# Gate and up products of an adaLN block's feed-forward: seven block products in place of eight, with its copies, splits and loads in a new order

## The chip, the core and the metric

One core of a Trainium2 chip runs the whole kernel in one launch. The metric is device time in microseconds (us), the median of three runs. The engines are PE (TensorE: matrix products, and PEld, its weight loads), DVE (VectorE), ACT (ScalarE), POOL (GpSimd) and SP (SyncE, which issues the DMAs). Each engine works through its own list of instructions in order; semaphores hold an instruction until another engine has signalled. SBUF is the on-chip memory of 128 partitions; PSUM, where PE puts its results, has 8 banks of 128 x 512 float32.

## The reference, cut to what matters

Four sequences of 512 tokens of width 512 go through an attention part (a gated delta rule with 6 heads) and then a feed-forward part:

```python
x = x + ga * attention(h)                       # h: normed, modulated x
h = _layernorm(x, axis=-1) * (1 + cb) + sb
gate = jnp.einsum('bsd,hd->bsh', h, w_gate)     # 2048 hidden units, 512 inputs
up   = jnp.einsum('bsd,hd->bsh', h, w_up)
gated = jax.nn.silu(gate) * up
x = x + gb * jnp.einsum('bsh,dh->bsd', gated, w_down)
```

All is float32. Both kernels make a float32 product out of three faster ones (type fp32r): each operand is split into a high part (a copy rounded to fp32r, made by ACT) and a low part (operand minus high part, made by DVE or POOL), and high x high, low x high and high x low are added up in one PSUM bank.

## The kernel before

**Order.** The program is a list of steps (`plan`), which each engine's function walks through, taking the parts that are its own. So the order of the `step(...)` calls is the order of every engine's list. Three stages matter here: projections and convolutions (to about 310 us of the trace), sixteen *units* of the recurrence (`slot_of(u)`, u = 0 to 15, to about 505 us), and the feed-forward.

**Units.** A unit works on 64 tokens of two sequences (`place(u)` gives the pair of sequences p and the chunk c; units 0, 1, 4, 5, 8, 9, 12, 13 belong to p = 0). Its output side is `po_sq`, `po_ln`, `po_os` (norm of the heads), `po_tr` (turn, gate, split), `po_wo` (18 matmuls by Wo), `po_yg`, `po_add`, `po_stat`, `po_xn`, which gives `XN1`, the normed rows for the feed-forward. SP writes them to `scrN` and the sum itself to `scrX`. PSUM banks 4 to 7 are handed out in two pairs by `take()` in turn.

**Feed-forward.** Hidden units are cut into 16 tiles j of 128; tokens into the four sequences b. For each j and b, `gu_gate` and `gu_up` are 4 x 3 matmuls each into one of banks 0 to 3 (`mm3`, line 1304): 64 x 24 = 1536 matmuls of 512 columns. ACT takes silu of the gate bank, DVE multiplies it with the up bank (`gated`), ACT and DVE split the result (FH, FL). `down` takes two j at a time: for each of the 4 token tiles s of b, 6 matmuls into a bank, which DVE adds into `YA`: 128 x 6 = 768 matmuls. Four banks are used for `down` after the first groups. The weights of tile j (gate, up, down side by side, 1536 columns) are loaded, split by one ACT copy and one DVE subtraction (`split_ff`), four tiles ahead of each other. The rows of tile n of XN1 come back from `scrN` (`load_xf`), are turned by PE (`c_turn`), scaled and shifted (`c_mod`) and split (`c_split`). POOL has next to nothing to do in the feed-forward until its end, where `out_pre` multiplies the sum by `gbB` and adds `scrX`; `gate_row` makes `gbB` by four plain float32 matmuls.

**What the change touches** is `split_ff` after units 10 and 13, `turn_unit`, `last_units`, `products`, `down` and `late_norms`, all inside `build`.

## Time and profile before

| | us |
|---|---|
| median of 3 runs (lowest, highest) | 1063.02 (1062.32, 1063.75) |
| the profiled execution, its own time | 1063.38 |
| its span, first to last instruction | 1061.6 |
| PE busy (share of the span) | 1022.6 (96%) |
| PEld, DVE, ACT, POOL busy | 822.1, 626.2, 375.0, 225.8 |
| mean granted clock of PE | 0.995 |

Busy time of PE is the time in which at least one matmul is under way; matmuls overlap, so their number times the distance from start to start says more than the busy share. The timeline shows merged stretches of equal instructions; the duration of such a row is that of the whole stretch.

### The profile page before, as it was taken

How to read it: one execution, taken by the hardware profiler on the slowest of the kernel's cores; microseconds unless marked ns; L12 is line 12 of the kernel's file. 1: busy time of each engine (PE TensorE's matmuls, PEld its weight loads, DVE VectorE, ACT ScalarE, POOL GpSimd, SP SyncE). 2: the span in 40 equal slices, each digit the busy share in tenths (PEclk: the TensorE clock that was granted, in tenths of full speed). 3: DMA queues.
4: the chain of work that ended last, by engine and by line, in shares of the span. 5: the costliest groups of instructions: out<-in, count | busy, mean ns of one | idle time of the engine just before them, and what ended most of it. 6: DMA issues, size and time to landing. Idle time of an engine off the chain costs nothing.

```text
span 1061.6 us, 20179 instructions
## 1 busy us (share of the span) xinstructions
PE 1022.6 (96%) x8112; PEld 822.1 (77%) x8112; DVE 626.2 (59%) x997; ACT 375.0 (35%) x685; POOL 225.8 (21%) x178
## 2 busy tenths in 40 slices
PE   6999999999998999998899999999999999999998
PEld 4676777777676888887777887888888888888886
DVE  5977377899855787878664333343333334334366
ACT  3676674445445343333453112211212212112110
POOL 1322530022025555554301000000000000004191
PEclk9999999999999999999999999999999999999999
...
GB/s 212 196 14 135 73 80 165 247 100 215 64 125 170 141 153 146 188 187 130 174 72 28 1 1 60 1 60 1 33 28 1 60 1 58 2 0 70 80 80 119
DMA packets 153438, 97.42 MB, mean 92 GB/s; under 512 B 93569, under 2 KB 130689, under 8 KB 153217
## 3 DMA queue, kind: packets, MB, share of 16 engines
...
## 4 chain that ended last, share of the span: by engine, by line
PE 73%; DVE 10%; DMA 5%; issue 4%; ACT 4%; SPq 4%; POOL 0%; DVEq 0%; ACTq 0%
PE ps L1302 70%; ACT t L1665 3%; PE ps L1310 3%; DVE t L1936 2%; DVE t L2046 2%; DMA scrU<-t 2%; SPq L1179 1%; DVE t L2034 1%; PE ps L1539 1%; DVE t L1941 1%; DVE t L2146 1%; DVE t L1946 1%; DMA scrA<-t 1%; SPq L1239 1%; DMA t<-scrA 1%
## 5 line engine op out<-in xcount | busy, mean ns | idle before, releaser
L1302 PE MATMUL ps<-t,t 128*128 128x512 f32 (+6 forms) x7292 | 969.7, 325 | 30.4 <-DVE t L1936 8.5
L1302 PEld LDWEIGHTS ps<-t,t 128*128 128x128 f32 (+4 forms) x7292 | 769.6, 159 | 215.1 <-issue 43.8
L1936 DVE TENSOR_TENSOR t<-ps,t 128x512 f32<-128x512 f32 (+2 forms) x288 | 199.6, 710 | 245.8 <-PE ps L1302 219.5
L1665 ACT ACTIVATE t<-t 128x512 fp32r<-128x512 f32 (+10 forms) x339 | 189.1, 579 | 308.8 <-DVE t L1936 206.2
L1936 DVE TENSOR_TENSOR t<-t,t 128x512 fp32r<-128x512 f32 (+14 forms) x210 | 168.1, 805 | 114.0 <-ACT t L1665 106.6
L1665 ACT ACTIVATE t<-ps 128x512 f32<-128x512 f32 (+5 forms) x202 | 109.1, 551 | 303.0 <-PE ps L1302 285.1
L2427 POOL TENSOR_TENSOR t<-t,t 128x512 f32<-128x512 f32 x16 | 22.5, 1408 | 375.2 <-DVE t L1936 373.1
L2046 DVE SCALAR_TENSOR_TENSOR t<-ps,t,t 128x511 f32<-128x511 f32 (+2 forms) x108 | 80.2, 747 | 3.3 <-ACT t L1665 0.5
L1665 ACT ACTIVATE t<-ps,t 128x512 f32<-128x512 f32 (+2 forms) x93 | 54.5, 617 | 26.1 <-PE ps L1310 13.0
L1310 PE MATMUL ps<-t,t 128*128 128x128 f32 (+1 forms) x340 | 52.3, 285 | 4.2 <-DVE t L1941 2.1
L1310 PEld LDWEIGHTS ps<-t,t 128*128 128x128 f32 (+1 forms) x340 | 38.1, 146 | 13.5 <-issue 5.5
L2406 POOL TENSOR_TENSOR t<-t,t 128x768 fp32r<-128x768 f32 x16 | 29.3, 1834 | 36.4 <-ACT t L1665 36.3
L2430 POOL TENSOR_TENSOR t<-t,t 128x512 f32<-128x512 f32 x16 | 22.7, 1417 | 40.6 <-DMA t<-scrX 38.6
L2362 POOL MEMSET t<- 128x3072 f32 x4 | 10.7, 2676 | 94.0 <-PE ps L1302 71.5
L2412 POOL TENSOR_TENSOR t<-t,t 128x512 f32<-128x512 f32 x16 | 20.7, 1296 | 44.3 <-DVE t L1936 44.1
L2332 POOL TENSOR_TENSOR t<-t,t 128x512 fp32r<-128x512 f32 x13 | 17.4, 1338 | 47.2 <-ACT t L1665 46.1
L1946 DVE BATCH_NORM_STATS2 t<-t 128x6 f32<-128x512 f32 x32 | 21.9, 684 | 8.4 <-DMA t<-in_x 6.8
L1941 DVE TENSOR_SCALAR t<-t,t,t 128x512 f32<-128x512 f32 x32 | 24.4, 768 | 2.1 <-ACT t L1665 1.9
L2343 POOL TENSOR_TENSOR t<-t,t 128x384 fp32r<-128x384 f32 x16 | 14.4, 900 | 52.7 <-PE ps L1302 32.7
L1665 ACT ACTIVATE t<-t,t 128x1 f32<-128x1 f32 (+2 forms) x36 | 13.2, 367 | 33.9 <-DVE t L1948 31.2
L2398 POOL TENSOR_TENSOR t<-t,t 128x768 f32<-128x768 f32 x16 | 23.6, 1473 | 2.7 <-POOL t L2412 2.4
L2034 DVE SCALAR_TENSOR_TENSOR t<-ps,t,t 128x510 f32<-128x510 f32 (+1 forms) x24 | 17.8, 744 | 5.8 <-ACT t L1665 5.4
...
## 6 DMA issues: line engine op xcount, KB each, us to landing
...
```

The costliest lines, as they stand in the source:

```text
L1302: return e.matmul(o, l, r_, start=start, stop=stop, skip_group_check=True)
L1310: return e.transpose(o, i, idn)
L1665: return e.activation(o, i, f, **kw)
L1936: return e.tensor_tensor(o, a, b, op)
L1941: return e.tensor_scalar(o, a, s1, s2, o1, o2)
L1946: e.bn_stats(st6[:, slot_, :], src).then_inc(sem(name + "bn"), 1)
L2034: e.scalar_tensor_tensor(yy[:, d + 1:SEQ], p_[:, 0:SEQ - d - 1], cwt[:, j, 2 - d:3 - d], yy[:, d + 1:SEQ], ALU.mult, ALU.add).then_inc(sem ...
L2046: e.scalar_tensor_tensor(yy[:, d + 1:SEQ], p_[:, 0:SEQ - d - 1], cwt[:, j, 2 - d:3 - d], yy[:, d + 1:SEQ], ALU.mult, ALU.add).then_inc(sem ...
L2398: signal(e.tensor_tensor(heads(Sg[:, :, :]), heads(S[:, 6 * pp:6 * pp + 6, :]), bc(decay, 3, [128, 2, 3, 128]), ALU.mult), "p_sg")
L2406: signal(e.tensor_tensor(OZl[:, :, :], OZ[:, :, :], OZh[:, :, :].bitcast(f32), ALU.subtract), "p_ozl")
L2427: signal(e.tensor_tensor(ya(b, s), ya(b, s), gbB[:, b, :], ALU.mult), "p_out")
L2430: signal(e.tensor_tensor(ya(b, s), ya(b, s), xo(b, s), ALU.add), "p_out")
```

## The change

The 2048 hidden units are taken in 8 blocks of 256, the tokens in two halves (sequences 0 and 1, then 2 and 3), which gives 16 iterations (`it`, half it // 8). In each, gate and up are one product of a 256 x 512 weight block by 512 x 1024 tokens, each side cut in 2 x 2, by Strassen's scheme in Winograd's form: seven products of 128 x 256 by 256 x 512, each 6 matmuls, instead of eight. A weight block needs three combinations and four blocks as they are (7 x 256 columns), made by four POOL instructions (`w_comb`), split by one ACT copy (`w_high`) and one POOL subtraction (`w_low_ff`). The tokens' seven operands (`HSh`, `HSl`, 1024 columns each) are made once in each half: `t_raw` on POOL, `t4` on DVE, and `split_h`.

The products `prod(n, o)`, n = 2 it for gate and 2 it + 1 for up, o = 0 to 6, add up in three banks (0 to 2 for gate, 3 to 5 for up). Three times ACT copies the first bank's running sum (`copy_s`), and the products that follow go on adding to the bank; DVE adds the copies to the other banks (`cadd`). `down` keeps banks 6 and 7 alone, which it also shares with `c_turn` and `gate_row`.

The rows of the first half are turned and modulated in the units (`turn_unit`: 4 transposes, and 8 DVE instructions of 64 columns), not loaded from `scrN`; those of the second half in iterations 1 and 2. The first half's output is finished in iteration 8 (`post_0`, `store_0`), the second's at the end. The weights are loaded twice, once in each half. The `split_ff` of gate, up and down by ACT and DVE is gone.

```diff
+        if u in (3, 4, 7, 8, 11, 12):
+            turn_unit(u - 3)
+        if u == 15:
+            turn_unit(13)
...
+    GU = [(1, 0), (2, 1), (6, 0), (5, 2), (7, 0), (4, 0), (3, 2)]
...
     def turn_unit(u):
...
+        p, free = take()
+        step("c_turn", u=u, bank=4 + 2 * p, free=[free])
+        t = tick("norm_tr")
+        unit_turned[u] = [t]
+        step("c_mod_unit", u=u, bank=4 + 2 * p, turned=t[1])
+        pfree(p, tick("v_cmod"))
...
+    def ring_bank():
+        i = 6 + yb["n"] % 2
+        yb["n"] += 1
+        return i, ring_free.get(i, [("v_yg", 16), ("v_cmod", 8), ("v_s", 16)])
...
         if u == 8:
-            step("load_ff", j=0, wait=("rec_d", 9))
+            w_load(0, 0, [("rec_d", 9)])
+        if u == 9:
+            w_comb(0)
         if u == 10:
-            step("split_ff", j=0)
-            step("load_ff", j=1, wait=("v_glo", 1))
+            w_high(0, [("rec_d", 8)])
+        if u == 12:
+            w_load(1, 0, [w_low_ff(0, [("rec_d", 12)])])
         if u == 13:
-            step("split_ff", j=1)
+            w_comb(1)
+            w_high(1, [("rec_d", 12)])
         if u == 14:
...
+            t_raw(0, 384, [("pr_kq", 16), ("v_kd", 16), ("v_cmod", 6)])
...
+    split_h(0, 0, [("pr_kq", 16), ("v_kd", 16)])
+    t_raw(384, 512, [("v_cmod", 8)])
+    w_low_ff(1, [("pr_kq", 16), ("v_kd", 16)])
...
+    step("po_sq", u=15)
+    prod(0, 0)
+    split_h(0, 1, done_r)
...
+    def next_gate(it, free):
+        w_high(gate_m(it + 1), free)
+        tok = w_low_ff(gate_m(it + 1))
...
+    def iteration(it):
+        n, last, turn = 2 * it, it == 15, it == 7
+        if it:
+            prod(n, 0)
+            prod(n, 1)
+            copy_s(n, 0)
+            flush()
+            prod(n, 2)
+            cadd(n, 0)
+            prod(n, 3)
+            copy_s(n, 1)
+            step("silu", it=it, t=0)
+            prod(n, 4)
+            down(it - 1, 0)
+            copy_s(n, 2)
+            cadd(n, 1)
+            w_high(up_m(it), [("prod", 7 * (n - 1) + 7)])
...
+        if not last:
+            w_comb(gate_m(it + 1))
+        for k in range(1, 7):
+            if it and (it < 15 or k < 4):
+                down(it - 1, k)
+            if it in (1, 2) and k in (1, 2, 3, 4):
+                turn_tile(4 * it - 4 + k - 1)
...
+            if it and not last and k == 3:
+                next_gate(it, [("prod", 7 * n + 7)])
...
+        if it == 4:
+            t_raw(0, 512, [("a_cmod", 8), ("v_hs", 8), ("a_hs", 7)])
...
+        if it and not last:
+            down(it - 1, 7)
+        copy_s(n, 2)
+        cadd(n, 1)
...
+        else:
+            split_h(1, 5, [("prod", 7 * n + 6)], "p")
+            split_h(1, 6, [("prod", 7 * n + 7)])
+            w_comb(up_m(it + 1))
+            cadd(n, 2)
+            for t in range(3):
+                gated(it, t)
+                fh(it, t)
+            w_high_d(it)
...
+                for kk in range(2):
+                    mm(dst, ah[kk], HSh[j][:, kk, :], kk == 0 and o in (0, 1, 3), False)
+                    mm(dst, al[kk], HSh[j][:, kk, :], False, False)
...
+                for kk in range(2):
+                    t = mm(dst, ah[kk], HSl[j][:, kk, :], False, kk == 1)
+                t.then_inc(sem("prod"), 1)
...
+                tt(dst[:, :], bank(3 * up + (1, 2, 2)[i]), SP_[(0, 2, 1)[i]][:, :], ALU.add).then_inc(sem("v_c"), 1)
...
+                signal(e.tensor_tensor(r_[:, 4, :], r_[:, 0, :], r_[:, 3, :], ALU.add), "p_ws")
...
+                signal(e.tensor_tensor(WGl[m % 3][:, :, :], WR[st["slot"]][:, :, :], WGh[m % 3][:, :, :].bitcast(f32),
+                                       ALU.subtract), "p_wl")
```

What this makes of three places. First, DVE in the middle of the feed-forward. Before, one group of two hidden tiles and one sequence (`<-ps,t_178` multiplies the up bank with silu, `<-t_180,...` is the low part, `t_186` and `t_187` are sums of `down`):

```order
L1936 TENSOR_TENSOR t_180<-ps,t_178 128x512 [waits v_fl,a_si,gu_up]
L1936 TENSOR_TENSOR t_196<-t_180,t_192 128x512 [waits a_fh,down]
L1936 TENSOR_TENSOR t_180<-ps,t_179 128x512 [waits v_fl,a_si,gu_up]
L1936 TENSOR_TENSOR t_197<-t_180,t_193 128x512 [waits a_fh,down]
L1936 TENSOR_TENSOR t_186<-ps,t_186 128x512 [waits v_y,down]
L1936 TENSOR_TENSOR t_187<-ps,t_187 128x512 [waits v_y,down]
```

After, the up half of an iteration from the seventh `down` on (`t_243`, `t_244`: sums of `down`; `t_231`, `t_232`, `t_234`: bank plus copy, that is `cadd`; `t_217<-t_231,t_217` gated; `t_225`, `t_226` low parts):

```order
L2117 TENSOR_TENSOR t_243<-ps,t_243 128x512 [waits v_y,down]
L2117 TENSOR_TENSOR t_231<-ps,t_210 128x512 [waits down,prod,a_sp]
L2117 TENSOR_TENSOR t_217<-t_231,t_217 128x512 [waits v_c,a_si]
L2117 TENSOR_TENSOR t_225<-t_217,t_219 128x512 [waits a_fh]
L2117 TENSOR_TENSOR t_244<-ps,t_244 128x512 [waits v_y,down]
L2117 TENSOR_TENSOR t_232<-ps,t_212 128x512 [waits down,prod,a_sp]
L2117 TENSOR_TENSOR t_218<-t_232,t_218 128x512 [waits v_c,a_si]
L2117 TENSOR_TENSOR t_213<-ps,t_213 128x512 [waits prod,a_si]
L2117 TENSOR_TENSOR t_234<-ps,t_211 128x512 [waits down,prod,a_sp]
L2117 TENSOR_TENSOR t_214<-t_234,t_214 128x512 [waits v_c,a_si]
L2117 TENSOR_TENSOR t_226<-t_218,t_220 128x512 [waits a_fh]
```

Three additions of a copy stand between the others, and the sum of the eighth `down` (`t_244`) stands right ahead of the second addition (`t_232`), for which PE's last product waits.

Second, ACT between units 13 and 14. Before (`t_73` is the row statistic of `po_stat`, `t_184<-t_181` is `split_ff`, `t_150` and `t_151` belong to the next unit's keys, `t_161` is `po_sq`):

```order
L1665 ACTIVATE t_73<-t_73 128x1 [waits a_p]
L1665 ACTIVATE t_184<-t_181 128x1536 [waits d_ff,rec_d]
L1665 ACTIVATE t_150<-t_60 128x384 [waits pr_q,pr_t]
L1665 ACTIVATE t_151<-t_70 128x384
L1665 ACTIVATE t_161<-ps 128x768 [waits v_red,rec_o]
```

After (`t_183<-t_178` is `w_high(1)`):

```order
L1809 ACTIVATE t_73<-t_73 128x1 [waits a_p]
L1809 ACTIVATE t_183<-t_178 128x1792 [waits p_ws,rec_d]
L1809 ACTIVATE t_150<-t_60 128x384 [waits pr_q,pr_t]
L1809 ACTIVATE t_151<-t_70 128x384
L1809 ACTIVATE t_161<-ps 128x768 [waits v_red,rec_o]
```

The copy stands at the same place; where it waited for a DMA (`d_ff`), it now waits for POOL's four combinations (`p_ws`), which are in POOL's list after the same unit.

Third, ACT where the halves change over, iteration 7 to 8, after only (before has no such place). `t_201` and `t_202` are the last two high parts of the second half's operands, `t_219` to `t_221` high parts of the gated values, `t_186` those of the down weights, `t_210<-ps` is the first `copy_s` of iteration 8:

```order
L1809 ACTIVATE t_201<-t_195 128x1024 [waits v_hs,a_cmod,prod]
L1809 ACTIVATE t_202<-t_193 128x1024 [waits a_cmod,prod]
L1809 ACTIVATE t_219<-t_217 128x512 [waits down,v_gf]
L1809 ACTIVATE t_220<-t_218 128x512 [waits down,v_gf]
L1809 ACTIVATE t_221<-t_213 128x512 [waits down,v_gf]
L1809 ACTIVATE t_186<-t_180 128x512 [waits down,d_ff]
L1809 ACTIVATE t_186<-t_181 128x512
L1809 ACTIVATE t_210<-ps 128x512 [waits v_c,prod]
```

The copy that frees iteration 8's first bank is the last of eight, and five of them wait for DVE.

## Rows read from the trace of the kernel before

**Rows 1.** Page, part 1: engine, busy us, share of span, instructions.

```profile
PE 1022.6 (96%) x8112; PEld 822.1 (77%) x8112; DVE 626.2 (59%) x997; ACT 375.0 (35%) x685; POOL 225.8 (21%) x178
```

**Rows 2.** Busy time by stretch: PE, PEld, DVE, ACT, POOL (instructions); clock; DMA.

```profile
675.00:700.00 25.00, 25.00 (x112) 20.69 (x111) 8.40 (x11) 4.31 (x6) 0.00 (x0) 1.00 0.09 31
```

**Rows 3.** Groups by form, PE, 517 to 1062 us: busy us, mean ns, idle.

```profile
L1302 PE MATMUL ps<-t,t 128*128 128x512 f32 x2322 | 531.5, 391 | 3.1 <-DVE t L1936 1.6 <-DVE t L2305 0.9 <-ACT t L1665 0.7
```

**Rows 4.** Timeline from 770 us: start, duration, engine, line, count.

```profile
769.82 36.43 PE L1302 MATMUL ps<-t,t 128*128 128x512 f32 x160
...
772.59 2.48 DVE L1936 TENSOR_TENSOR t<-ps,t 128x512 f32<-128x512 f32 x4
```

**Rows 5.** Timeline, 0.05 us at 785.2: last matmul, next one, the waiting multiplication.

```profile
785.01 0.61 PE L1302 MATMUL ps<-t,t 128*128 128x512 f32 x2
...
785.21 0.69 DVE L1936 TENSOR_TENSOR t<-ps,t 128x512 f32<-128x512 f32 x1 [3.23 <-PE ps L1302]
```

**Rows 6.** Timeline at 550 us: two bank copies, and PE waiting for the first.

```profile
549.81 1.28 DVE L2305 COPY t<-ps 128x512 f32<-128x512 f32 x2
...
550.55 1.19 PE L1302 MATMUL ps<-t,t 128*128 128x512 f32 x4 [0.24 <-DVE t L2305]
```

**Rows 7.** Groups by form, whole span: mean ns by number of columns.

```profile
L1936 DVE TENSOR_TENSOR t<-t,t 128x1536 fp32r<-128x1536 f32 x16 | 28.8, 1801 | 38.8 <-ACT t L1665 38.8
...
L1665 ACT ACTIVATE t<-t 128x1536 fp32r<-128x1536 f32 x16 | 23.7, 1481 | 58.3 <-DMA t<-in_wf 54.2 <-PE ps L1302 4.0
...
L1665 ACT ACTIVATE t<-ps 128x512 f32<-128x512 f32 x95 | 55.9, 596 | 211.6 <-PE ps L1302 194.3 <-DMA scrU<-t 17.0
...
L2382 POOL TENSOR_TENSOR t<-t,t 128x384 fp32r<-128x384 f32 x16 | 13.3, 830 | 11.6 <-PE ps L1302 9.5 <-POOL t L2406 0.4
...
L2372 POOL TENSOR_TENSOR t<-t,t 128x1024 fp32r<-128x1024 f32 x3 | 7.1, 2361 | 8.6 <-ACT t L1665 8.6
```

**Rows 8.** Timeline at 513 us: two DVE subtractions beside POOL's.

```profile
513.60 3.08 DVE L1936 TENSOR_TENSOR t<-t,t 128x512 fp32r<-128x512 f32 x2
...
514.63 1.50 POOL L2412 TENSOR_TENSOR t<-t,t 128x512 f32<-128x512 f32 x1 [0.17 <-POOL t L2418]
```

**Rows 9.** Timeline of PE, 300 to 520 us: one step that every unit has.

```profile
468.26 0.87 PE L1539 MATMUL ps<-t,t 128*128 128x128 f32 x6
480.06 0.88 PE L1539 MATMUL ps<-t,t 128*128 128x128 f32 x6
492.50 0.88 PE L1539 MATMUL ps<-t,t 128*128 128x128 f32 x6
```

**Rows 10.** Timeline between units 13 and 14: `split_ff`'s low part, `pr_gm`, `po_sq`.

```profile
481.80 2.12 DVE L1936 TENSOR_TENSOR t<-t,t 128x1536 fp32r<-128x1536 f32 x1 [0.18 <-ACT t L1665]
...
482.38 2.22 POOL L2385 TENSOR_TENSOR t<-t,t 128x384 fp32r<-128x384 f32 x1
...
482.49 0.79 ACT L1665 ACTIVATE t<-ps 128x768 f32<-128x768 f32 x1
```

**Rows 11.** Timeline, start of the feed-forward: turning, modulating, first products.

```profile
505.50 0.66 PE L1310 MATMUL ps<-t,t 128*128 128x128 f32 x4
...
507.68 2.11 DVE L1941 TENSOR_SCALAR t<-ps,t 128x64 f32<-128x64 f32 x8
...
509.66 1.49 ACT L1665 ACTIVATE t<-ps,t 128x128 f32<-128x128 f32 x4
...
517.04 9.93 PE L1302 MATMUL ps<-t,t 128*128 128x512 f32 x42 [1.55 <-DVE t L1936]
```

**Rows 12.** Timeline at the end: an addition beside POOL, the last addition, last matmuls.

```profile
1022.78 1.07 DVE L1936 TENSOR_TENSOR t<-t,t 128x512 f32<-128x512 f32 x1
...
1058.47 0.69 DVE L1936 TENSOR_TENSOR t<-t,t 128x512 f32<-128x512 f32 x1
...
1055.65 1.52 PE L1302 MATMUL ps<-t,t 128*128 128x512 f32 x6
```

**Rows 13.** Busy time by stretch, columns as in rows 2: after the four `gate_row`.

```profile
642.00:644.00 2.00, 2.00 (x5) 1.63 (x6) 0.00 (x0) 0.00 (x0) 0.00 (x0) 0.50 0.53 163
```

More of the change, by code:

```diff
@@ L858, in evict_gu @@
-    def evict_gu(kind, i, j, n, fs):
-        if kind == "gate":
-            step("silu", bank=i, n=n)
-            return
-        k = n % 4
-        held = f_free[k] if k in f_free else [low[i_] for i_ in F_TILES[k]]
-        step("gated", bank=i, n=n, f=k, held=held)
-        fs.append((k, j, n))
-    first_fs = []
-    ahead_of = {}
-    def side_15():
-        yield
-        mod_unit(*turn_unit(12))
-        yield
-        ahead_of[13] = turn_unit(13)
-        for n, at_bank in ((0, None), (1, 0), (2, 1)):
-            ahead_of[n] = turn(n, at_bank)
-        yield
@@ new lines, in build, with w_load, w_comb, w_high @@
+    count.update(d_w0=160, d_w1=144)
+    comb_at, high_at = {}, {}
+    def w_load(m, slot, free):
+        step("w_load", m=m, slot=slot, free=free)
+        ff_raw[m] = slot, tick(f"d_w{slot}", 16)
+    def w_comb(m):
+        step("w_comb", m=m, slot=ff_raw[m][0], loaded=ff_raw[m][1])
+        comb_at[m] = tick("p_ws", 4)
+    def w_high(m, free):
+        step("w_high", m=m, slot=ff_raw[m][0], free=free + [comb_at[m]])
+        high_at[m] = tick("a_wh")
+    w_low_at = {}
+    def w_low_ff(m, free=()):
+        step("w_low_ff", m=m, slot=ff_raw[m][0], free=list(free) + [high_at[m]])
+        w_low_at[m] = tick("p_wl")
+        return w_low_at[m]
@@ new lines, in cadd, with f_of, f_held @@
+    def cadd(n, i):
+        step("cadd", n=n, i=i)
+        tick("v_c")
+    def f_of(it, t):
+        return {1: 4, 3: 5}.get(t, t) if it == 15 else t
+    def f_held(it, t):
+        if it == 0 or f_of(it, t) > 3:
+            return []
+        return [("down", 8 * (it - 1) + (4 if t in (0, 2) else 8))]
+    yb = {"n": 0}
+    ring_free = {}
+    def ring_bank():
+        i = 6 + yb["n"] % 2
+        yb["n"] += 1
+        return i, ring_free.get(i, [("v_yg", 16), ("v_cmod", 8), ("v_s", 16)])
@@ new lines, in down, with gate_row, turn_tile @@
+    def down(it, k):
+        i, free = ring_bank()
+        step("down", it=it, k=k, bank=i, free=free)
+        tick("down")
+        ring_free[i] = [tick("v_y")]
+        if it == 7:
+            step("post_0", k=k)
+        if it == 14:
+            step("out_pre", k=k)
+    def gate_row(b):
+        i, free = ring_bank()
+        step("gate_row", b=b, bank=i, free=free)
+        ring_free[i] = [tick("a_grow")]
+    def turn_tile(n):
+        i, free = ring_bank()
+        step("c_turn", n=n, bank=i, free=free)
+        t = tick("norm_tr")[1]
+        step("c_mod", n=n, bank=i, turned=t)
+        ring_free[i] = [tick("a_cmod")]
@@ new lines, in build @@
+    copy_s(0, 0)
+    ringed("po_tr", 15, ("v_oz", 16))
+    cadd(0, 0)
+    split_h(0, 3, done_r)
+    prod(0, 2)
+    split_h(0, 4, done_r)
+    step("po_yg", u=14)
+    step("po_add", u=14)
+    copy_s(0, 1)
+    prod(0, 3)
+    split_h(0, 5, done_r)
+    ringed("po_wo", 15, ("v_yg", 16))
+    split_h(0, 6, done_r)
+    step("po_stat", u=14)
+    step("po_xn", u=14)
+    prod(0, 4)
+    copy_s(0, 2)
+    step("po_yg", u=15)
+    step("po_add", u=15)
+    cadd(0, 1)
+    prod(0, 5)
+    prod(0, 6)
@@ new lines, in build, with gate_m, up_m, flush @@
+    step("po_stat", u=15)
+    step("po_xn", u=15)
+    cadd(0, 2)
+    step("table", set="silu_and_others")
+    for t in range(3):
+        step("silu", it=0, t=t)
+    step("w_load_d", it=0, free=[("po_wo", 16), ("p_x1", 16)])
+    step("load_xf", n=0)
+    step("load_xf", n=1)
+    def gate_m(it):
+        return 3 * it
+    def up_m(it):
+        return 3 * it + 1
+    late = []
+    def flush():
+        while late:
+            late.pop(0)()
+    def gated(it, t):
+        step("gated", it=it, t=t)
@@ new lines, in w_load_next, with w_high_d @@
+    def w_load_next(it, tok):
+        if it < 15:
+            w_load(up_m(it + 1), 1, [tok])
+    def w_high_d(it):
+        high = tick("a_wh")
+        step("w_high_d", it=it, hi=high)
+        tok = tick("p_wl")
+        w_low_at[3 * it + 2] = tok
+        if it < 15:
+            step("w_load_d", it=it + 1, free=[tok])
+    for it in range(16):
+        if it == 8:
+            step("load_x1")
+        if it == 10:
+            step("load_xo", ks=(0, 1, 2, 3, 4, 5))
+        iteration(it)
@@ L1025, in build @@
+    flush()
+    for k in range(4, 8):
+        down(14, k)
+    for k in range(8):
+        down(15, k)
     step("end")
```

807 lines of the change are left out of this document (439 added, 368 removed).

## The prediction

> **What bounds the kernel now.** I read the page's busy shares first: PE 96%, DVE 59%, POOL 21% [rows 1]. A share hides stages, so next come the busy times by stretch: in the feed-forward PE is busy in all of a 25-us stretch, 112 matmuls in it, at granted clock 1.00, and POOL does nothing [rows 2]. The groups by form say where PE's idle time in this part lies: some 6 us in all, ended by DVE and ACT [rows 3], so at the start. After 575 us only the number of matmuls counts. The timeline gives their price: a merged run of 160 lasts 36.43 us, and a matmul outlasts its start by about 0.39 [rows 3, 4], so one starts each (36.43 - 0.39) / 159 = **0.2267 us**, and a group of six takes 1.36.
>
> The closer timeline gives what a handover costs. A new group starts at 785.01, and DVE's read of the bank just finished starts at 785.21, so 0.20 later [rows 5]. DVE needs 0.69 for a bank, and successive ones start each (2.48 - 0.69) / 3 = 0.60 [rows 4, 5]. A bank copied from 549.81 on, 0.69 long, lets PE go on at 550.55, so 0.05 later [rows 6]. Before, all this is hidden by four banks for sums and four for products.
>
> **The change, part by part.** The sum is made against the profiled run, 1063.38; the median lies 0.36 below it.
>
> *Removed.* Matmuls of gate and up: 1536 to 1344, same shape, 192 x 0.2267 = **-43.5**. All lie on the path [rows 2].
>
> *Prices of the new pieces* [rows 7]: POOL 0.83 for 384 columns and 2.36 for 1024, so 2.4 ns a column; 0.52 for a combination of 256, 4.2 for a low part of 1792. ACT 1.48 for 1536, so about 1.75 for 1792 and 1.0 for 1024; 0.60 for a bank. DVE 1.80 for 1536, so 1.2 for 1024. DVE with two SBUF operands beside POOL is held until POOL's instruction ends: two that take some 1.2 together took 3.08 [rows 8]; one of 0.6 took 1.07 [rows 12]; one that reads PSUM isn't held. POOL is held in turn: 384 columns took 2.22 beside DVE's split [rows 10].
>
> *The recurrence's loop.* Units start each 11.80 us; after unit 13, with DVE's 2.12 of `split_ff`, the pitch is 12.44 [rows 9, 10]. So 2.12 on DVE cost 0.64, and 1.5 was covered. Six turned units add 4 transposes (0.66) and 2.11 of DVE [rows 11], the same kind of burden: 0 to 0.64 each, I take 0.4, +2.5. After unit 12, `w_low_ff(0)` occupies POOL for 4.2 and holds the small DVE products of `po_ln`: 0 to 4, I take 4.0 - 1.5, +2.5. The old split's 0.64 goes. After unit 13, ACT's `w_high(1)` waits for POOL's four combinations behind `pr_gm`, which ends at 484.60 [rows 10]: 484.6 + 2.1 + 1.75 = 488.4, and `po_sq`, two ACT instructions later, starts at about 489.3 instead of 482.49. That is 6.8 late, of which 1.5 is covered: +5.3, between 2 (if the unit's other half hides more) and 6.8. `t_raw` at unit 14 +0.5. Queued behind the waiting ACT copy are `po_sq` and the next keys, and PE, DVE wait for both. Sum **+10.2**, 4 to 16.
>
> *Start of the feed-forward.* From 505.50 [rows 11] to the last matmuls' end at 1057.17 [rows 12] are 551.7 us; 2340 matmuls (2304, and 36 of `po_wo`) make 530.5, transposes and the gate rows with their clock dip about 11 [rows 11, 13], so PE waits some 10.4 before. After, DVE's list sets the first seven products: 7 x 1.2 low parts, 1.2 for `t4`, and up to 4.2 of holding by POOL's `w_low_ff(1)`: 13.8 beside 9.5 of products. Two more handovers follow: the seventh product waits for `cadd` behind `po_yg`, the next gate's first copy for three silus. Walking the three lists with these prices gives 13.7 of waiting, 3.3 more than before; 24 transposes have moved into the loop, -2.2. **+1.1**, -4 to +6.
>
> *The steady half-iterations.* Product 7 waits for `cadd(1)`, and in DVE's list this stands right behind the sum of a `down` that ended one group earlier. So from the end of that `down` pass 0.20 + 0.60 + 0.69 + 0.05 = 1.54, for a group of 1.36: a wait of 0.2, 28 times, and 0.9 at the two where no `down` stands between. **+6.5**; nothing if DVE reads the bank's first columns earlier, 14 if POOL's holding doubles each wait.
>
> *Turning tiles in iterations 1 and 2.* With two banks, a `down` behind a `turn_tile` waits for the sum before it: 0.20 + 0.69 + 0.05 = 0.94, less the turning's 0.36, so 0.6, four times, and 0.6 more where `c_mod` is behind `w_high`: 3.0 twice, 6.0. The gate rows lose 0.7 likewise, and the clock dip after them (0.50 for a while, [rows 13]) may not return: -1.5. **+5.2**, 0 to 8.
>
> *The change-over.* In iteration 7's second half all seven operands are remade. Counted from the end of the last product: ACT's high part 1.0, DVE's low part 1.2, `cadd` 0.69, three `gated` 2.0, ACT's last `fh` 0.5, two `w_high_d` 1.0, then the `copy_s` for which PE's third product of iteration 8 waits, 0.6: 7.0, less two products, 2.7: a wait of 4.3. Three of DVE's instructions take two SBUF operands and POOL makes low parts of 1024 columns at this time: each may add 2.36. I take two, 9.0 in all, of 4.3 to 11.4. In iteration 8, `post_0` adds a multiplication on DVE behind every sum: 0.69 + 1.07 - 1.36 = 0.4, eight times, 3.2; iteration 4's `t_raw` 0.8. **+13.0**, 5 to 18.
>
> *The end.* The last sums are each followed by a multiplication and an addition shared between POOL and DVE, 1.7 beside 1.36: eight times 0.34; and `down(14, 6)` waits behind `gated` and low parts, 1.3. **+4.0**, 1 to 5.5.
>
> *At nothing:* POOL's 8.3 x 2 of weight work an iteration (POOL is empty there, and an iteration's 22 groups last 30 us), silu and `fh` on ACT (about 10 of 30), and the second load of the weights (DMA share 0.09 [rows 2]). If that cover is gone, the third case below gives the price.
>
> **Sum:** -43.5 + 10.2 + 1.1 + 6.5 + 5.2 + 13.0 + 4.0 = -3.5: 1059.9 by the profiled run, **1059.5** on the median's scale. The seven terms' bounds vary apart from each other: 1052 to 1067 for this case.
>
> **A rule against the change.** In this trace PE waits several times for a bank between 549 and 570 us and the one dip of the feed-forward's clock is behind the four gate rows, where it is 0.50 of full, that is 1.2 instead of 2.4 GHz [rows 13]. A clock that fell once in each iteration, and halved a group of 1.36, would add 1.4 to 1.7 x 16, so 25: 1085.
>
> The Trainium skill's page "TensorE: Matmul & The Clock Gate", section "A second HAM failure mode: psum-queue depth-cycling", says that a kernel whose matmul groups cycle through PSUM banks with small idle times between them can see the clock swing between its levels. This trace does not show it for waits of 0.2 to 0.7 us; by that rule the time would be the one just given.
>
> **Rivals.**
> 1. *The edges overlap.* Terms from the loop to the end were added as if each wait reached PE whole. If engines run ahead at the edges, they go half the way or more down to their lower bounds, for the loop, the start, the steady part, the tiles, the change-over and the end: 6 + (-1) + 3 + 2.5 + 8 + 2.5 = 21, so -22.5: **1040.5**. For it: 2.12 on DVE cost only 0.64. Against it: at the change-over and after unit 13 the lists leave no other order.
> 2. *POOL's chain comes late (slower).* In an iteration POOL makes `w_low` of up, then four combinations, ACT copies them high, POOL makes `w_low` of the next gate: 4.2 + 2.1 + 1.75 + 4.2, with handovers. By my walk it ends 22.6 us after the iteration's start, just where DVE wants `gated(0)` (22.9), which has two SBUF operands and is held as in [rows 8]. DVE has 1.9 of room behind it. When the chain is over 20% longer, ends after 24.8, the sum of `down` 8, `cadd(1)` and product 7 come late in each of 14 iterations. At 1.3 times the price: (3.4 - 2.2) x 14 = 16, **1076**. For it: POOL's 2.22 for 0.83 of work [rows 10], since DVE is busy all through. Against it: the plain prices [rows 7] leave room.
> 3. *The clock swings*, 1085, as above.
> 4. *The change doesn't do what it says:* the lists hold 2112 matmuls of 512 columns in the feed-forward, so only a longer pitch could undo the gain; at 2% more (0.0045), 2112 x 0.0045 = 9.6, **1069**.
>
> **How the numbers follow.** Forecast 0.47, rival 1 0.25, rival 2 0.18, the clock 0.05, a longer pitch 0.05. The predicted time is the forecast's. The range reaches from just below rival 1 to just above rival 2, 1038 to 1079: outside are the clock and the outer parts of rivals 1 and 2, about 0.2. A measurement of this kernel tells about 0.2% from no change, so same is 1060.9 to 1065.1: of the forecast 0.27 lies below it, 0.10 in it, 0.10 above; with the rivals faster 0.52, same 0.12, slower 0.36.
>
> **What the profile after would show.** The step on matmuls holds if their pitch stays 0.2267 and the granted clock 1.00. The steady term: waits of PE for DVE of about 0.2 once in a half-iteration, behind the sum of a `down`. The loop: a gap on ACT ended by POOL near 485, `po_sq` near 489, and unit 14 to 15 some 5 us longer. The change-over: PE's longest wait, some 9 us, ended by ACT's bank copy. The POOL rival: long DVE subtractions and `gated` that end with POOL's low part, in every iteration. The forecast is wrong if waits at the edges sum to under 25 or over 55 us, or if each iteration has one of over 1 us.

## The result and the profile after

| | before | after |
|---|---|---|
| median (lowest, highest), us | 1062.72 (1062.32, 1063.75) | 1088.72 (1084.48, 1090.98) |
| ratio, 95% interval | | 1.0239 (1.0206 to 1.0271) |
| span of the profiled execution | 1061.6 | 1082.7 |

The change makes the kernel **slower by 26 us**, where 3.5 less was forecast; 1088.7 lies above the range. The profiled execution is the fastest of the four.

The page of after, part 1, against [rows 1]: PE is busy 15 us less, and POOL 283 more.

```profile
PE 1007.7 (93%) x7920; PEld 787.9 (73%) x7920; DVE 704.1 (65%) x1106; ACT 482.8 (45%) x827; POOL 509.0 (47%) x366
```

Busy time by stretch of after, columns as in [rows 2]: the full stretch is still full, at granted clock 1.00; two others are not.

```profile
525.00:550.00 25.00, 18.09 (x67) 13.26 (x68) 19.31 (x21) 10.30 (x17) 11.01 (x8) 0.86 0.21 64
...
800.00:825.00 25.00, 19.27 (x72) 15.03 (x73) 17.72 (x21) 8.15 (x13) 13.86 (x10) 0.86 0.38 127
...
900.00:925.00 25.00, 25.00 (x108) 19.94 (x108) 13.29 (x20) 11.82 (x17) 12.49 (x10) 1.00 0.18 63
```

Groups by form of after, PE from 525 us on; the last number of each kind is idle time ahead, by what ended it. Against the 3.1 us of [rows 3] there are 36.5, ended by ACT, DVE and POOL:

```profile
L1413 PE MATMUL ps<-t,t 128*128 128x512 f32 x2120 | 508.6, 398 | 36.5 <-ACT t L1809 16.0 <-DVE t L2117 13.6 <-POOL t L2646 4.8
```

The timeline of PE in after. L1650 is the step of [rows 9]; it comes once in each slot, that is, in each turn of the loop of units (slot 13 goes from 466.22 to 482.64, slot 14 to 502.97); the other rows end PE's long waits.

```profile
466.22 0.87 PE L1650 MATMUL ps<-t,t 128*128 128x128 f32 x6
...
475.80 1.28 PE L1413 MATMUL ps<-t,t 128*128 128x384 f32 x5 [2.42 <-DVE t L2117]
...
482.64 0.88 PE L1650 MATMUL ps<-t,t 128*128 128x128 f32 x6
...
491.85 0.58 PE L1413 MATMUL ps<-t,t 64*64 64x64 f32 x24 [3.30 <-ACT t L1809]
...
495.81 1.46 PE L1413 MATMUL ps<-t,t 128*128 128x384 f32 x5 [2.90 <-DVE t L2117]
...
502.97 0.87 PE L1650 MATMUL ps<-t,t 128*128 128x128 f32 x6
...
512.17 0.89 PE L1413 MATMUL ps<-t,t 64*64 64x128 f32 x24 [2.85 <-DVE t L2117]
...
529.01 1.22 PE L1413 MATMUL ps<-t,t 128*128 128x512 f32 x2 [4.26 <-DVE t L2117]
...
559.49 15.63 PE L1413 MATMUL ps<-t,t 128*128 128x512 f32 x66 [3.36 <-ACT t L1809]
...
802.40 9.36 PE L1413 MATMUL ps<-t,t 128*128 128x512 f32 x30 [7.71 <-ACT t L1809]
...
822.20 5.80 PE L1413 MATMUL ps<-t,t 128*128 128x512 f32 x24 [2.60 <-DVE t L2117]
...
849.56 197.99 PE L1413 MATMUL ps<-t,t 128*128 128x512 f32 x832 [3.96 <-POOL t L2646]
```

These marks cut both programs into the same stretches:

| stretch, us | before | after | difference | forecast |
|---|---|---|---|---|
| start to the first L1650 (L1539 before) | 313.66 | 308.20 | -5.5 | 0 |
| thirteen slots to 466.22 (468.26) | 154.60 | 158.02 | +3.4 | +2.5 |
| slot 13 | 11.80 | 16.42 | +4.6 | +2.5 |
| slot 14 | 12.44 | 20.33 | +7.9 | +4.7 |
| from there to the end of the last matmul | 564.67 | 575.59 | +10.9 | -13.2 |

The first line has nothing to do with the change: that stretch took 308.5 to 314.8 in the other kernels below, 312.4 in one that differs from the kernel before only in its feed-forward. So the differences of stages say more than the totals of two profiles. Of the thirteen slots' 3.4, 1.5 lie in the second, which the change doesn't touch. The six slots with a turned unit take 12.13 to 12.23 where a plain one takes 11.80, 2.5 together; one of them has lost the old split's 0.64.

What the waits have in common is seen on DVE and POOL. Timeline of after around four of them: POOL's low part of 1792 columns, and the DVE instruction that started beside it (ahead of the last one stands what POOL did before it, and its wait).

```profile
469.53 4.03 POOL L2639 TENSOR_TENSOR t<-t,t 128x1792 fp32r<-128x1792 f32 x1 [0.17 <-POOL t L2594]
...
470.67 2.91 DVE L2117 TENSOR_TENSOR t<-t,t 128x6 f32<-128x6 f32 x1
...
523.83 3.98 POOL L2639 TENSOR_TENSOR t<-t,t 128x1792 fp32r<-128x1792 f32 x1 [0.17 <-POOL t L2657]
...
523.95 5.00 DVE L2117 TENSOR_TENSOR t<-t,t 128x6 f32<-128x6 f32 x2
...
553.74 4.01 POOL L2639 TENSOR_TENSOR t<-t,t 128x1792 fp32r<-128x1792 f32 x1
554.00 4.29 DVE L2117 TENSOR_TENSOR t<-t,t 128x512 f32<-128x512 f32 x1
...
815.27 1.29 POOL L2670 TENSOR_TENSOR t<-t,t 128x512 f32<-128x512 f32 x1 [9.94 <-DMA t<-scrX]
...
816.71 4.29 POOL L2639 TENSOR_TENSOR t<-t,t 128x1792 fp32r<-128x1792 f32 x1
...
817.75 3.80 DVE L2117 TENSOR_TENSOR t<-t,t 128x512 f32<-128x512 f32 x1
```

A product of six columns, 0.17 in before, takes 2.91 and ends with POOL's instruction, at 473.6; one of 512 columns, 0.69 alone, takes 4.29 and ends 0.54 after POOL's. So DVE is held until POOL has done, as in [rows 8], and 2.4 to 4.3 us of PE's waiting stand behind each. DVE's additions that read a PSUM bank aren't held: 156 of them beside POOL take 0.69 on average, as without it.

And behind the waits the clock falls. Busy time by stretch of after, PE alone (busy, granted clock, DMA):

```profile
476.00:478.00 2.00, 2.00 (x16) 0.50 1.01 313
478.00:480.00 2.00, 2.00 (x30) 0.65 1.04 192
480.00:482.00 2.00, 2.00 (x80) 1.00 0.06 15
```

Of the nine waits above, 2.42, the pair of 3.30 and 2.90, 2.85, 4.26, 7.71 and 3.96 are followed by such a stretch, 3.36 and 2.60 are not. Busy time of PE times the missing share of the clock, summed over windows of 1 us from 470 us on, is 12.9 us in after and 1.7 in before (the gate rows of [rows 13]). The forecast's sum had no term for it.

### The profile page after: what moved, and what is told of

The parts are those of the page before. It is cut to its first block and busy times, and to the rows that moved or that the text cites. A ratio compares the mean times of both kernels' runs of the same rounds, so it can differ in the third digit from the quotient of the medians.

```text
span 1082.7 us, 20418 instructions
## 1 busy us (share of the span) xinstructions
PE 1007.7 (93%) x7920; PEld 787.9 (73%) x7920; DVE 704.1 (65%) x1106; ACT 482.8 (45%) x827; POOL 509.0 (47%) x366
## 5 line engine op out<-in xcount | busy, mean ns | idle before, releaser
L1413 PE MATMUL ps<-t,t 128*128 128x512 f32 (+7 forms) x7100 | 952.6, 328 | 69.2 <-DVE t L2117 23.7
L1413 PEld LDWEIGHTS ps<-t,t 128*128 128x128 f32 (+4 forms) x7100 | 734.6, 161 | 273.3 <-issue 57.3
L1809 ACT ACTIVATE t<-t 128x512 fp32r<-128x512 f32 (+11 forms) x433 | 273.1, 650 | 251.8 <-DVE t L2117 144.4
L2117 DVE TENSOR_TENSOR t<-ps,t 128x512 f32<-128x512 f32 (+2 forms) x336 | 231.0, 706 | 225.8 <-PE ps L1413 162.8
L1809 ACT ACTIVATE t<-ps 128x512 f32<-128x512 f32 (+5 forms) x250 | 138.2, 560 | 260.7 <-PE ps L1413 244.5
L2117 DVE TENSOR_TENSOR t<-t,t 128x512 fp32r<-128x512 f32 (+14 forms) x247 | 210.9, 875 | 45.2 <-ACT t L1809 33.5
L2639 POOL TENSOR_TENSOR t<-t,t 128x1792 fp32r<-128x1792 f32 x32 | 130.5, 4079 | 122.4 <-ACT t L1809 121.3
L2646 POOL TENSOR_TENSOR t<-t,t 128x512 fp32r<-128x512 f32 x32 | 47.8, 1514 | 47.4 <-ACT t L1809 46.9
L2571 POOL MEMSET t<- 128x3072 f32 x4 | 10.7, 2674 | 92.1 <-PE ps L1413 70.0
L1421 PEld LDWEIGHTS ps<-t,t 128*128 128x128 f32 (+1 forms) x340 | 38.6, 147 | 10.9 <-issue 4.3
L2621 POOL TENSOR_TENSOR t<-t,t 128x512 f32<-128x512 f32 x16 | 21.5, 1341 | 49.9 <-DVE t L2117 49.7
L2552 POOL TENSOR_TENSOR t<-t,t 128x384 fp32r<-128x384 f32 x16 | 14.1, 884 | 52.6 <-PE ps L1413 32.6
L2541 POOL TENSOR_TENSOR t<-t,t 128x512 fp32r<-128x512 f32 x13 | 17.4, 1339 | 44.4 <-ACT t L1809 43.3
L1809 ACT ACTIVATE t<-t,t 128x1 f32<-128x1 f32 (+2 forms) x36 | 13.2, 367 | 39.9 <-DVE t L2129 36.1
L2633 POOL TENSOR_TENSOR t<-t 128x256 f32<-128x256 f32 x32 | 27.1, 847 | 2.5
L2629 POOL TENSOR_TENSOR t<-t 128x256 f32<-128x256 f32 x32 | 26.8, 838 | 2.5
L2627 POOL TENSOR_TENSOR t<-t 128x256 f32<-128x256 f32 x32 | 25.2, 787 | 4.9 <-POOL t L2639 0.4
```

Of the source, the lines that this page charges most:

```text
L1413: return e.matmul(o, l, r_, start=start, stop=stop, skip_group_check=True)
L1421: return e.transpose(o, i, idn)
L1809: return e.activation(o, i, f, **kw)
L2117: return e.tensor_tensor(o, a, b, op)
L2621: signal(e.tensor_tensor(YB[u % 2][:, :], YB[u % 2][:, :], XB[u % 2][:, :], ALU.add), "p_x1")
L2627: signal(e.tensor_tensor(r_[:, 4, :], r_[:, 0, :], r_[:, 3, :], ALU.add), "p_ws")
```

## The experiments

Theory A: what the forecast left out is that POOL's low parts hold DVE where PE depends on it, and that a long wait of PE is paid again at half clock. Theory B: the orders of the lists do it, with the plain durations. Each kernel is compared with the kernel before on its own chip.

**e5: the price of a wait alone**, in the kernel before (POOL counts `p_x1` up when its multiplications are done):

```diff
...
+            if jj == 1 and 2 <= q < 7:
+                step("stall", n=n, reps=(1, 2, 3, 5)[b], first=not stalls)
+                stalls.append(n)
+                ready = [("p_x1", 16 + len(stalls))]
             step("gu_gate", j=j, b=b, bank=i1, free=gu["free"][i1] + ready, n=n)
...
```

> The kernel before the change, with 20 waits put into PE's list in the feed-forward's full stretch, 27 us apart: before the second gate product of each group in q = 2 to 6, PE waits until POOL, which starts when the up product ahead has ended, has done 1, 2, 3 or 5 multiplications of 512 columns (b = 0 to 3) on a scratch tile. By POOL's 1.29 for such an instruction and 0.17 between two, PE waits about 1.6, 3.0, 4.5 and 7.4 us, five times each, 83 us in all. Theory A (a long wait is paid a second time at half clock): stretches at granted clock 0.50 of 3 to 8 us follow the waits of 4.5 and 7.4 and perhaps of 3.0, none the 1.6; each costs about half its length, so the time rises by 83 and 15 to 30 more. Theory B (half clock in the changed kernel had another cause): granted clock stays at 1.00 and the time rises by 83 alone.

1157.42 in one run, 96.6 above the kernel before. Timeline of PE: a stretch of 72 matmuls after each wait (its length is the second number, the wait stands in brackets).

```profile
666.17 16.61 PE L1308 MATMUL ps<-t,t 128*128 128x512 f32 x72 [1.23 <-issue]
685.12 18.20 PE L1308 MATMUL ps<-t,t 128*128 128x512 f32 x72 [2.34 <-issue]
706.78 17.96 PE L1308 MATMUL ps<-t,t 128*128 128x512 f32 x72 [3.46 <-ACT t L1671]
...
768.81 16.60 PE L1308 MATMUL ps<-t,t 128*128 128x512 f32 x72 [2.34 <-issue]
...
812.83 19.47 PE L1308 MATMUL ps<-t,t 128*128 128x512 f32 x72 [6.02 <-issue]
```

Busy time by stretch of PE behind the second wait:

```profile
685.00:687.00 2.00, 1.88 (x6) 0.72 0.00 0
687.00:689.00 2.00, 2.00 (x6) 0.50 0.00 0
689.00:691.00 2.00, 2.00 (x10) 0.93 0.00 0
```

16.6 is the length at full clock. Idle of 1.22 was followed by no half clock in five cases, 2.34 in three of five, 3.46 and 6.02 in all ten. The stretch behind is then 1.3 to 2.9 longer. The rows behind the second wait give its price: the missing shares of the clock, 0.28, 0.50 and 0.07 of 2 us each, are 1.7 us of work, and the stretch is 1.6 longer. Over the nineteen waits that end from 685.12 to 1067.32: from 666.17 on, 401.15 us exceed 19 x 72 x 0.2267 by 91.0; 64.0 of them are idle, 3.1 the part of each wait that the modelled end of a matmul covers (0.39 - 0.23 each), and 23.9 are left for the twelve slow stretches (by their lengths, 21.9). Theory A's second half holds, here where PE sets the pace: **a long wait costs its length and some 2 us more**.

The Trainium skill's page "TensorE: Matmul & The Clock Gate", section "HAM oscillation — how this bites in real kernels", describes a kernel whose bursts of products each begin at the lower clock because of the wait ahead of them, and counts half of the slow time as lost. The rows behind the second wait agree, with 1.7 us of work lost and a stretch that is 1.6 longer.

**e1: POOL's low parts in seven pieces**

```diff
...
-                in_order()
-                signal(e.tensor_tensor(WGl[m % 3][:, :, :], WR[st["slot"]][:, :, :], WGh[m % 3][:, :, :].bitcast(f32),
-                                       ALU.subtract), "p_wl")
+                for c in range(7):
+                    in_order()
+                    signal(e.tensor_tensor(WGl[m % 3][:, c, :], WR[st["slot"]][:, c, :],
+                                           WGh[m % 3][:, c, :].bitcast(f32), ALU.subtract), "p_wl" if c == 6 else "p_ws")
```

> The changed kernel, with each of POOL's low parts of 1792 columns (4.03 us) cut into seven of 256, so that a DVE instruction with two SBUF operands waits at most for one piece. Theory A (holding): such an instruction beside a low part of POOL took 2.91 instead of 0.17 in slot 13, 5.00 for two at the feed-forward's start, 4.29 in iteration 0 and 3.80 in iteration 8, and PE waited 2.42, 4.26, 3.36 and 2.60 behind them, the first two followed by half clock: with the pieces the four waits shrink to under 1.2 each and the time falls by 8 to 14 us. Theory B (order of the lists alone; DVE would have been late anyway): falls by less than 3, or rises, since POOL then needs some 5.7 instead of 4.1 for each low part.

1094.09, ratio 1.0311 (1.0252 to 1.0370): no gain. Timeline of e1, at the places of the rows of after, then PE's longest wait and the longest low part:

```profile
476.29 5.61 POOL L2641 TENSOR_TENSOR t<-t,t 128x256 fp32r<-128x256 f32 x7 [0.17 <-POOL t L2595]
...
477.44 0.44 DVE L2118 TENSOR_TENSOR t<-t,t 128x6 f32<-128x6 f32 x1
...
529.33 1.76 DVE L2118 TENSOR_TENSOR t<-t,t 128x6 f32<-128x6 f32 x2
...
814.14 9.65 PE L1414 MATMUL ps<-t,t 128*128 128x512 f32 x30 [10.07 <-ACT t L1810]
...
827.82 8.59 POOL L2641 TENSOR_TENSOR t<-t,t 128x256 fp32r<-128x256 f32 x7
```

On DVE the theory is right at the places named: 2.91 became 0.44, 5.00 became 1.76, 4.29 became 1.00, and slot 13 took 12.40 instead of 16.42. PE's waits shrank less than expected: at the start of the feed-forward 1.00, 2.05 and 2.62 stand for 4.26 and 1.00. The pieces take POOL 5.6 us alone and up to 8.6 beside DVE, and where POOL itself is waited for all comes later: the wait in the change-over grew from 7.71 to 10.07, a wait for the down weights from 3.96 to 5.79, another in iteration 4 from 0.89 to 4.08. Besides, the stretch ahead of the recurrence took 314.8 in this profile, 308.2 in after's. So the total didn't test the theory; e9 does.

**e2: the weights' copy behind `rec_d`'s**

```diff
         if has_rec:
             step("rec_d", u=u)
+        if u == 14:
+            w_high(1, [("rec_d", 12)])
...
             w_comb(1)
-            w_high(1, [("rec_d", 12)])
```

> The changed kernel, with ACT's high part of the second weights, w_high(1), moved in ACT's list from ahead of po_sq of unit 13 to behind the copy of rec_d in the next slot; POOL's combinations stay. Forecast's price of this place: 5.3. Theory A (a long wait of PE is paid a second time at half clock): the slot from one rec_v to the next, 20.33 us there and 12.44 before the change, falls to 13 or less, 7 to 8 us, and the stretch at granted clock 0.50 behind the waits of 3.30 and 2.90 goes. Theory B (the wait alone): falls by 5 to 6.

1079.29, ratio 1.0160 (1.0106 to 1.0215): 9 less than after. Slot 14 took 11.80 instead of 20.33: 8.5, where the waits' 6.2 and the missing clock's 2.0 make 8.2. The forecast's 5.3 was the wait, with the slack taken off that the next unit doesn't have, and without the clock. In the same kernel slot 13 shows the clock's price by chance: the same wait of 2.4 was not followed by half clock, and the slot took 14.89 instead of 16.42.

**e4: `cadd(1)` ahead of the sum of `down`**

```diff
             prod(n, 4)
-            down(it - 1, 0)
             copy_s(n, 2)
             cadd(n, 1)
+            down(it - 1, 0)
```

and the same for `down(it - 1, 7)`; PE's list stays.

> The changed kernel, with cadd(1) ahead of the sum of the neighbouring down in DVE's list, in both halves of every iteration; PE's, ACT's and POOL's lists are unchanged. Forecast's step: 0.2 at each of 28 places, so 5.6 less. By the steady iteration as measured (30.67 us for 22 groups of 1.360, 29.93): 0.75 in each of some 14 iterations, so 10 less, and the iteration falls to 30.0. Rival (the waits have another cause, POOL holding DVE): no change, iteration stays at 30.67.

1078.20, ratio 1.0146 (1.0100 to 1.0193): 10 less; the feed-forward took 566.97 instead of 575.59. POOL's low parts of the up weights, one in each iteration, give the period. After, then e4:

```profile
885.32 4.07 POOL L2639 TENSOR_TENSOR t<-t,t 128x1792 fp32r<-128x1792 f32 x1 [7.80 <-ACT t L1809]
...
915.99 4.06 POOL L2639 TENSOR_TENSOR t<-t,t 128x1792 fp32r<-128x1792 f32 x1 [7.81 <-ACT t L1809]
...
946.70 4.06 POOL L2639 TENSOR_TENSOR t<-t,t 128x1792 fp32r<-128x1792 f32 x1 [7.82 <-ACT t L1809]
```

```profile
882.16 4.07 POOL L2639 TENSOR_TENSOR t<-t,t 128x1792 fp32r<-128x1792 f32 x1 [7.42 <-ACT t L1809]
...
912.33 4.07 POOL L2639 TENSOR_TENSOR t<-t,t 128x1792 fp32r<-128x1792 f32 x1 [7.42 <-ACT t L1809]
...
942.49 4.07 POOL L2639 TENSOR_TENSOR t<-t,t 128x1792 fp32r<-128x1792 f32 x1 [7.42 <-ACT t L1809]
```

30.69 became 30.17: one addition queued behind a sum, the mechanism forecast, cost 0.26 in each half-iteration, where 0.2 was forecast. 132 matmuls at 0.2267 are 29.93, and the 0.24 that e4 leaves is no wait. Its timeline of PE over that iteration is one row without idle time:

```profile
882.01 30.56 PE L1413 MATMUL ps<-t,t 128*128 128x512 f32 x133
```

One matmul starts each (30.56 - 0.39) / 132 = 0.2286 us, 0.8% more than the 0.2267 of [rows 4]. What makes the pitch longer is not shown.

**e3: the change-over's copy moved ahead** (iteration 7's `gated`, `fh` and `fl` go into `rest`, which `flush` calls)

```diff
             copy_s(n, 0)
-            flush()
+            if it != 8:
+                flush()
...
             copy_s(n, 1)
+            flush()
...
-            for t in range(3):
-                gated(it, t)
-                fh(it, t)
             w_high_d(it)
...
```

> The changed kernel, with the change-over in another order: iteration 7's gated products, high and low parts move behind the second bank copy of iteration 8, so that the first copy of iteration 8 stands right behind the last high part of the operands in ACT's list. Queue theory: PE's wait of 7.71 behind that copy falls under 2, a new wait of 1 to 3 comes before iteration 8's first down sums, and the time falls by 4 to 7, by 2 more if the half clock that followed (802 to 807 us) goes too. Rival: the operands' own split on DVE and POOL is the limit, and the wait only moves to a later product: falls by less than 2.

1085.10, ratio 1.0211 (1.0165 to 1.0256), not told apart from after. Timeline of PE, then busy time by stretch (PE, PEld, DVE, ACT, POOL) of e3:

```profile
796.72 4.37 PE L1415 MATMUL ps<-t,t 128*128 128x512 f32 x18 [1.53 <-ACT t L1811]
806.09 13.50 PE L1415 MATMUL ps<-t,t 128*128 128x512 f32 x48 [5.00 <-DVE t L2119]
```

```profile
795.00:800.00 5.00, 3.47 (x15) 2.74 (x15) 4.82 (x5) 2.54 (x6) 4.70 (x4) 1.00 0.01 2
800.00:805.00 5.00, 1.09 (x5) 0.56 (x3) 5.00 (x5) 4.49 (x7) 4.61 (x4) 0.91 0.00 0
```

The wait of 7.71 is split into 1.53 and 5.00. From iteration 7's low part to iteration 10's e3 takes 115.8 (770.31 to 886.13), after 115.5 (769.82 to 885.32), so nothing was gained at the place itself. ACT's order was only the last link: DVE and POOL are full. The rival is right.

**e6 and e7: the repairs together.** e6 is e2 and e4, with the low parts of weights 0, 1 and 3 alone cut, and `turn_unit(12)` moved:

```diff
-        if u == 15:
-            turn_unit(12)
...
         if u == 15:
+            turn_unit(12)
             turn_unit(13)
```

e7 adds e3's order and, around iteration 8, three steps at other places (they are taken out where they stood):

```diff
+            step("load_x1")
             w_high_d(it)
...
             w_load_next(it, w_low_ff(up_m(it)))
+            if it == 8:
+                step("post_0", k=0)
...
             w_high_d(it)
+            if it == 8:
+                w_comb(up_m(it + 1))
```

> The changed kernel with four edits outside the change-over: w_high(1) behind rec_d's copy as in e2; cadd(1) ahead of the down sum as in e4; the first three low parts that caught DVE (weights 0, 1 and 3) cut in seven, the others whole; turn_unit(12), whose eight DVE instructions stand ahead of the subtraction for which rec_d of unit 15 waits (PE waits 2.85), moved behind it to turn_unit(13). Expected from the places: 9.4 (e2) + 10.5 (e4) + 4.0 of slot 13 + 2.5 to 4 of the start and iteration 0 + 2 to 4 of slot 15: 28 to 32 less than the changed kernel's 26 above the kernel before, so a ratio of 0.995 to 1.000. Rival (a wait taken away at one place comes back at the next, as the cut low parts showed in the change-over): half of it, ratio about 1.010.

> As e6, with the change-over changed too: order of e3; the loads of scrX issued ahead of the next down weights; POOL's first addition of post_0, which waited 9.94 us for such a load, behind POOL's low part of the up weights; POOL's combinations for iteration 9 behind the low part of the down weights, for which PE waited 3.96 us in iteration 9. If DVE's full list (4.8 and 5.0 of 5 us busy from 795 to 805 in e3) is the limit of the change-over: only the 3.96, its half clock and some of the 2.60 go, 5 to 7 less than e6. If POOL's waiting for the load set iteration 8: 8 to 12 less than e6.

e6: 1063.48, ratio 1.0028 (1.0012 to 1.0044), 25 less than after; slots 13 and 14 took 12.41 and 11.81. A little short of the range expected: the start gave back less, since `turn_unit(12)` now stands in another wait (1.66 before the first products). e7: **1053.80, ratio 0.9936 (0.9912 to 0.9960)**, faster than both kernels. Timeline of PE in e7's change-over, all waits over 1 us:

```profile
778.83 5.97 PE L1420 MATMUL ps<-t,t 128*128 128x512 f32 x18 [1.90 <-ACT t L1816]
788.20 4.26 PE L1420 MATMUL ps<-t,t 128*128 128x512 f32 x12 [3.39 <-DVE t L2124]
```

It is 9.7 below e6, in the 8 to 12 that were expected if POOL's waiting for the load had set iteration 8. Here e3's order pays, together with POOL's list freed of the wait for `scrX` (9.94 us in after, ahead of the low part that held DVE at 817.75): the 2.60 and the 3.96 are gone. The moves were made together; what each of them is worth is not shown. From iteration 7's low part to iteration 10's, after takes 115.5, e7 102.75 (752.59 to 855.34); three steady iterations are 92.1 and 90.5. So 23.4 were lost in after, 12.2 in e7. That this equals the forecast's 12.2 (13.0 without the 0.8 of iteration 4) is chance: the forecast was for the other order.

**e9: e7 with the three low parts whole again**

```diff
-                cuts = [slice(c, c + 1) for c in range(7)] if m in (0, 1, 3) else [slice(0, 7)]
+                cuts = [slice(0, 7)]
```

> As e7, but with the low parts of weights 0, 1 and 3 whole again, one POOL instruction of 4.03 us each. Theory A (holding): slot 13 goes back from 12.40 to 16.4, the 5.00 of the two small DVE products at the feed-forward's start and the 4.29 of gated in iteration 0 return, with PE's waits of about 4 and 3 and a half clock behind the first: 8 to 11 more than e7's 1053.8. Theory B (the held instructions were covered; only the lists' orders counted): 0 to 3 more.

1061.85, ratio 1.0016 (0.9988 to 1.0044): 8 more than e7, and the intervals lie apart. Slot 13 took 14.88, without the half clock of after. Timeline of PE in e9: the waits are back.

```profile
477.40 0.84 PE L1418 MATMUL ps<-t,t 128*128 128x384 f32 x5 [2.41 <-DVE t L2122]
...
522.16 0.73 PE L1418 MATMUL ps<-t,t 128*128 128x512 f32 x2 [3.88 <-DVE t L2122]
...
552.29 15.36 PE L1418 MATMUL ps<-t,t 128*128 128x512 f32 x66 [3.33 <-ACT t L1814]
```

By place, e9's profile is 2.5 longer in slot 13, 4.0 from there to the fourth low part (564.41, in e7 556.75), 1.4 in the second slot, which no edit touches, and the same behind (489.5 and 489.2 to the last matmul). Of the 4.0 at most 1.7 is a half clock behind the 3.88, which e7 doesn't have there; the hold alone is the larger part. So three cuts among 32 low parts are worth 6.5 us by place and 8 by the medians, all 32 (e1, without the other repairs) nothing: theory A's first half holds where DVE is waited for and POOL is not.

**e8: the wait filled with matmuls**, ahead of the third product of iteration 8

```diff
...
+            elif kind == "fill":
+                for i in range(28):
+                    mm(bank(st["bank"]), WGh[0][:, 0, 0:128], HSh[0][:, 0, :], True, True)
```

> The changed kernel with 28 matmuls of 512 columns (6.35 us) put into PE's list where it waits 7.71 us for the first bank copy of iteration 8; they write a bank of the down ring that is free then and is started anew by the next down, so nothing that is used changes, and the copy comes when it came. Theory A (the half clock of 802 to 807 us is the price of PE's idle time): the wait shrinks to about 1.2, the granted clock stays at 1.00, the 30 matmuls behind it take 7.1 instead of 9.36 us, and the period of the up weights' low part from iteration 7 to 8 and on to 9 falls by up to 2.3. Theory B (the half clock comes from something else in the change-over): dip and 9.36 stay.

1087.08 in one run, as after. Timeline of PE in e8:

```profile
784.76 17.88 PE L1416 MATMUL ps<-t,t 128*128 128x512 f32 x76 [0.26 <-ACT t L1817]
804.07 7.42 PE L1416 MATMUL ps<-t,t 128*128 128x512 f32 x30 [1.43 <-ACT t L1817]
```

The half clock is gone and the 30 matmuls take 7.42 instead of 9.36, as theory A says. Yet from iteration 7's low part to iteration 10's e8 takes 116.4 (771.42 to 887.84), after 115.5: the waits that follow the filled one grew, to 2.77, 1.85 and 2.21 where after has 2.60, 0.46 and 1.49. The price of e5 is paid only where PE sets the pace afterwards; in the change-over DVE does.

## Why the prediction was wrong

Two steps failed. The term for the change-over took iteration 8 as paying for `post_0`'s multiplications alone, and was 11 short. And every wait of PE was priced at its length, less what was taken as covered: the half clock behind six long waits had no term, nor did the low parts that held DVE at two more places.

- **The matmuls removed: right.** e4's iteration has 132 matmuls in 30.17; before, the same part of the work is 144 x 0.2267 = 32.6. But the pitch, taken as unchanged, is 0.2286 in that iteration; for all matmuls that makes, as an estimate, 2112 x 0.0019 = 4.0 us that the sum put at nothing. Rival 4, a longer pitch, is right in kind, at 0.8% instead of 2%.
- **Six turned units: right.** 2.5 of the six slots, as forecast. The old split stood in two slots (12.44 in both, 11.80 in a plain one); the forecast took 0.64 off once.
- **Slots 13 and 14: right in place and cause, too small.** 4.6 and 7.9 for 2.5 and 4.7. Both times 1.5 were taken off as covered, on the strength of DVE's 2.12 having cost 0.64 [rows 9, 10], and half clock was not counted. e1 and e2 put the two at 4.0 and 8.5.
- **Steady half-iterations: right cause and nearly right size.** 0.52 x 14 = 7.3 for 6.5. Another 0.24 x 14 = 3.3 is the longer pitch.
- **Turning tiles:** 571.62 to 642.78, less two steady iterations and eight turnings of 0.36, is 6.9 for 6.0: right.
- **The start of the feed-forward: wrong.** The held instructions were counted once, on the split of the operands. Not counted: that the same low part holds the two small products of `po_ln` (5.00), and that the next one holds `gated` of iteration 0 (4.29). The visible waits from 505 to 560 us sum to 14.6, near the 13.7 forecast, in part by luck: 2.85 of them are a wait for the recurrence's last slot, which the walk of the lists didn't have. 4.2 of missing clock come on top and no slack was there to take them.
- **The change-over: the largest miss**, 23.4 for 12.2. The wait behind the last operand came, 7.71 for 9.0, though ACT's queue, by which it was counted, was not what set it (e3). The step that failed is the next one, iteration 8 taken as paying for `post_0`'s multiplications alone: 3.2 was forecast, and five waits of 9.2 together came, with half clock on top. In the trace POOL first waits 9.94 for `scrX`, its low part comes late and holds DVE (2.60 at PE), and then the down weights' low part comes late (3.96); e7, which moves that wait along with other steps, has neither. That is the mechanism of rival 2, at one place instead of in fourteen iterations.
- **Rival 2 in the steady part: wrong, narrowly.** POOL's second low part ends at 898.67 in after, and the multiplication that it would have held starts at 899.28.
- **The rival of the clock: right that it falls, wrong in when.** It named small waits, one in each iteration, and gave 1085 by that. Two small waits in each iteration, 0.26 each, leave the granted clock at 1.00 from 885 to 1010 us; it was the single long waits, six times, 12.9 us of work in all. That 1085 lies near the result is chance. The Trainium skill's page "TensorE: Matmul & The Clock Gate", section "A second HAM failure mode: psum-queue depth-cycling", which the prediction cites, tells of a clock that swings when groups of matmuls cycle through PSUM banks with small idle times between them. This trace does not show it, as the 1.00 above says.
- **Rival 1, edges that overlap: wrong.** No term that was measured came out near its lower bound.
- **At nothing: right for most.** ACT and the second load of the weights were hidden. POOL's weight work was hidden in the steady iterations only.

The sign that the prediction named, waits at the edges over 55 us, did not come: PE's 36.5 from 525 us on and the four waits ahead of them sum to 48. Half clock and a longer pitch, the other part of the miss, don't show in a sum of waits.

So some 30 us separate forecast and result in the stages: 11 in the change-over, some 6 at the start (what the other terms leave of the last line's 24.1), 4 in the steady part (3 of it the pitch), 5 in the two slots, 1.6 in iteration 4 (`t_raw`, 2.4 for 0.8), and small ones. The missing clock is part of these, at most 11. Behind the 7.71 of the change-over, e8 shows, it wasn't what set the time.

What stays open: how the missing clock and the hold share the start's 6 in after itself (e9 shows them in another order); why the pitch is longer; what each move in e7's change-over is worth; and why the same wait is followed by half clock in one run and not in another.
